# A mixing product in quarters of the array, with POOL making one of its later terms

## The reference

```
x, B, C = silu(conv(norm(u) @ W_in))           # x: 64 tokens x 512 channels
Y[l, h, p] = sum_s  (C[l] . B[s]) * L[h, l, s] * (x[s, h, p] * dt[s, h])      # L: decay, 0 for s > l
y = Y + x * D[h]
y = rmsnorm(y * silu(z)) * norm_w @ W_out
```

## Time and profile before

| | |
|---|---|
| median of 3 runs | 1300.21 us |
| the profiled execution | 1300.34 us, its span 1298.4 us |
| TensorE busy | 1229.9 us, 95% |
| VectorE busy | 1031.4 us, 79% |
| POOL busy | 796.1 us, 61% |
| ScalarE busy | 703.5 us, 54% |
| mean granted clock of TensorE | 0.978 |
| mixing product (L1278), 512 records | 35.9 us busy |
| mask product (L911, L914), 32 each | 21.5 and 22.1 us busy |
| first half of the gate (L928), 128 operations | 35.9 us busy |

### The profile page before, as it was taken

How to read it: one execution, slowest core, us unless ns; L and a number is a source line. 1 busy time by engine, 2 the same in 40 slices (tenths; PEclk the granted TensorE clock), 3 DMA queues, 4 the chain that set the end, 5 groups by cost and what they waited for, 6 DMA issues and landing times.

```text
span 1298.4 us, 32119 instructions
## 1 busy us (share of the span) xinstructions
PE 1229.9 (95%) x10803; PEld 1024.4 (79%) x10803; DVE 1031.4 (79%) x2572; ACT 703.5 (54%) x1588; POOL 796.1 (61%) x1435
## 2 busy tenths in 40 slices
PE   4789999999999999999999999999999999999865
PEld 3677888888888888888888888888888888888743
DVE  3675888888888888888888888888888888888555
ACT  3564566555555655555565555556555555665432
POOL 3465666667666666766666676666667666666541
PEclk8799999999999999999999999999999999999986
DMA  8300000000000000000000000000000000000000
GB/s 272 112 13 13 10 14 18 16 12 16 16 8 12 16 16 12 16 16 8 12 16 16 12 16 16 9 11 16 16 12 16 16 12 8 12 14 13 6 5 9
DMA packets 30645, 28.62 MB, mean 22 GB/s; under 512 B 7696, under 2 KB 28944, under 8 KB 30352
## 3 DMA queue, kind: packets, MB, share of 16 engines
q1 hardware_dynamic: 27680, 28.11, 6.8%
q10 hardware_dynamic: 2928, 0.03, 0.1%
HBM read 23.93 MB, written 4.19 MB: 22 GB/s over the span
## 4 chain that ended last, share of the span: by engine, by line
PE 87%; DVE 5%; POOL 3%; issue 2%; ACT 1%; DMA 1%; POOLq 0%; DVEq 0%; SPq 0%; ACTq 0%
PE bank L1405 17%; PE bank L1315 16%; PE bank L1397 5%; PE bank L1238 5%; PE bank L1375 4%; PE bank L1288 4%; PE bank L1247 4%; PE bank L1278 3%; PE bank L1425 3%; PE bank L1210 2%; PE bank L1430 2%; PE bank L1328 2%; PE bank L1227 2%; PE bank L1443 2%; PE bank L1385 2%
## 5 line engine op out<-in xcount | busy, mean ns | idle before, releaser
L1315 PE MATMUL bank<-xcT,wq 128*128 128x128 f32 x2048 | 236.2, 276 | 1.6 <-ACT xcT L648 1.6
L1315 PEld LDWEIGHTS bank<-xcT,wq 128*128 128x128 f32 x2048 | 231.1, 192 | 6.2 <-issue 2.0
L1405 PE MATMUL bank<-wo,oT 128*128 128x256 f32 x1024 | 232.1, 380 | 0.0
L1405 PEld LDWEIGHTS bank<-wo,oT 128*128 128x128 f32 x1024 | 190.6, 191 | 23.9 <-issue 0.3
L877 DVE SCALAR_TENSOR_TENSOR xc<-bank,cw,xc 128x124 f32<-128x124 f32 (+2 forms) x576 | 163.9, 341 | 15.2 <-ACT xc L618 8.4
L663 ACT ACTIVATE qT<-bank,bqT 128x128 f32<-128x128 f32 x384 | 109.7, 369 | 47.1 <-PE bank L1315 46.8
L354 POOL TENSOR_SCALAR m_mv<-m_mv 128x1 f32<-128x1 f32 x32 | 7.7, 241 | 158.1 <-DVE m_mv L845 158.1
L422 POOL TENSOR_TENSOR rq<-rq,minus_half 128x16 f32<-128x16 f32 x32 | 93.1, 2909 | 7.8 <-DVE rq L975 7.8
L1031 DVE SCALAR_TENSOR_TENSOR h<-h,bank 128x512 f32<-128x512 f32 x64 | 44.1, 688 | 64.9 <-ACT h L702 64.9
L434 POOL TENSOR_TENSOR pr<-pr,mask 128x512 f32<-128x512 f32 x64 | 82.9, 1315 | 14.0 <-DVE pr L982 14.0
L444 POOL TENSOR_TENSOR pr<-pr,mx 128x512 f32<-128x512 f32 x64 | 65.4, 1044 | 40.3 <-DVE mx L994 40.3
(11 more groups left out here) (225 smaller groups left out, 3053.7 us busy)
## 6 DMA issues: line engine op xcount, KB each, us to landing
x_in<-in_x SPq DMA_DIRECT2D x32, 128.0 KB, 2.1
c_in<-in_ctx SPq DMA_DIRECT2D x32, 128.0 KB, 2.0
x_m<-in_x SPq DMA_DIRECT2D x32, 128.0 KB, 2.0
out<-x SPq DMA_DIRECT2D x32, 128.0 KB, 1.7
wq<-in_L_xattn_Wq SPq DMA_DIRECT2D x1, 2048.0 KB, 14.3
wo<-in_L_xattn_Wo SPq DMA_DIRECT2D x1, 2048.0 KB, 12.7
w_in<-in_L_attn_W_in SPq DMA_DIRECT2D x1, 1024.0 KB, 6.0
qT<-in_L_ffn_w_gate SPq DMA_DIRECT2D x1, 1024.0 KB, 9.4
```

What stands on the lines that cost most here:

```text
L1315: last = mm(x_Qbank[g][:, (n % 4) * P:(n % 4 + 1) * P], wq[:, c, n * HD:(n + 1) * HD], xcT[:, c, :], start=(c == 0), stop=(c == DC - 1))
L1405: last = mm(X1[:, 0:D], oT[:, n, :, :], wo[:, n, :], start=(n == 0), stop=(n == NH - 1))
```

## The change

- `mbd` (128 x 8 x 128 with its zeros) becomes `mw` (128 x 8 x 64), the same weights without zeros; one multiplication of all 128 partitions writes it, and it now waits for the product of the tile before. The fill at the start goes.
- The product is made in 16 pieces. Each takes the 64 rows of one sequence, 64 columns of `xdt` and 64 of `mw`; the four pieces of a pair of heads lie on the four quarters of the array. The first sequence's results go to the first half of bank `M0`, the second's to the second half of bank `M2`. TensorE increments a semaphore that nobody waits for between the waits and the first piece.
- x * D becomes a product of POOL (`m_skip`, 128 x 512, into `xd`), after the attention's scaling and before `f_scales`; the gate adds it in two operations, one for each sequence. POOL's wait for D's load moves up with it, and VectorE's goes.
- As `M2` now holds results, `x_sums` waits for `m_y` (the gate's addition) instead of `m_Xdt`.

```diff
-            g.memset(mbd[:], 0.0).then_inc(s["c_memset"].sem, 1)
-            pool.wait_ge(s["c_memset"].sem, 5)
+            pool.wait_ge(s["c_memset"].sem, 4)
...
+        m_mixed = [M0[:, 0:2 * P], M2[:, 2 * P:4 * P]]
...
+            def m_skip(t):
+                after(pool, s["m_xs"], t + 1)
+                after(pool, s["m_y"], t)
+                g.tensor_tensor(xd[:], xc[:, 0:XCH, :], bcast(d_ch[:, :].unsqueeze(2), [P, XCH, P]),
+                                ALU.mult).then_inc(s["m_xd"].sem, 1)
...
+                if first == 0:
+                    pool.wait_ge(s["w_skip"].sem, 16 * W_SKIP)
+                if m is not None:
+                    m_skip(m)
                 if f is not None:
                     f_scales(f)
...
-                v.tensor_tensor(mbd[0:SEQ, :, 0:SEQ], decay[0:SEQ, :, :],
-                                bcast(gm[0:SEQ, :].unsqueeze(1), [SEQ, NHM, SEQ]), ALU.mult)
-
-                v.tensor_tensor(mbd[SEQ:P, :, SEQ:P], decay[SEQ:P, :, :],
-                                bcast(gm[SEQ:P, :].unsqueeze(1), [SEQ, NHM, SEQ]), ALU.mult).then_inc(s["m_Ma"].sem, 1)
+                after(dve, s["m_Y"], t)
+                v.tensor_tensor(mw[:], decay[:], bcast(gm[:, :].unsqueeze(1), [P, NHM, SEQ]), ALU.mult).then_inc(s["m_Ma"].sem, 1)
...
-                for j in range(XCH):
-                    last = v.scalar_tensor_tensor(out=yT[:, j, :], in0=xc[:, j, :], scalar=d_ch[:, j:j + 1],
-                                                  in1=M0[:, j * P:(j + 1) * P], op0=ALU.mult, op1=ALU.add)
+                after(dve, s["m_xd"], t + 1)
+                for a in range(2):
+                    tokens = slice(a * SEQ, (a + 1) * SEQ)
+                    last = v.tensor_tensor(yT[:, :, tokens], m_mixed[a].rearrange("p (j l) -> p j l", j=XCH), xd[:, :, tokens], ALU.add)
...
-                for n in range(NHM):
-                    last = mm(M0[(n % 2) * HP:(n % 2 + 1) * HP, (n // 2) * P:(n // 2 + 1) * P], xdt[:, n, :], mbd[:, n, :],
-                              start=True, stop=True)
+                pe.sem_inc(s["p_waited"].sem, 1)
+                for j in range(XCH):
+                    for a in range(2):
+                        rows = slice(a * SEQ, (a + 1) * SEQ)
+                        for u in range(2):
+                            last = mm(m_mixed[a][u * HP:(u + 1) * HP, j * SEQ:(j + 1) * SEQ], xdt[rows, 2 * j + u, :],
+                                      mw[rows, 2 * j + u, :], start=True, stop=True)
...
-                    after(pe, s["m_Xdt"], m + 1)
+                    after(pe, s["m_y"], m + 1)
```

More of the change, by code:

```diff
@@ L131, in decoder_layer @@
         gm = sb("gm", [P, SEQ])
-        mbd = sb("mbd", [P, NHM, P])
+        mw = sb("mw", [P, NHM, SEQ])
+        xd = sb("xd", [P, XCH, P])
         xdt = sb("xdt", [P, NHM, HP])
@@ L200, in decoder_layer @@
           m_raw+m_rl+m_nabs m_u m_up+m_rec+m_ratio m_log m_dt+m_dtA m_dAh+m_dAl m_Rh+m_Rl m_seg m_E m_tz m_zs
-          m_tap m_convb+m_conva m_tb+m_ta m_bc+m_xs m_G m_Gm+m_Ma m_Xtr m_Xdt
+          m_tap m_convb+m_conva m_tb+m_ta m_bc+m_xs m_G m_Gm+m_Ma m_Xtr m_Xdt m_xd
           m_Y m_y+m_yf m_sq m_ssy m_v4+m_ry m_out m_x1
@@ L504, in body @@
                     pool.wait_ge(s["w_out_l"].sem, 16)
-                    pool.wait_ge(s["w_skip"].sem, 16 * W_SKIP)
                     g.tensor_tensor(w_out[:], w_out[:], bcast(nw[:, :].unsqueeze(2), [P, XCH, D]),
@@ L1114, in body @@
                     m_spread(ms)
-                if first == 0:
-                    dve.wait_ge(s["w_skip"].sem, 16 * W_SKIP)
                 if m is not None:
```

## The result

| | before | changed |
|---|---|---|
| median of the runs, us | 1299.91 (1298.71 to 1300.24, 4) | 1284.15 (1283.53 to 1285.03, 4) |
| ratio, 95% interval | | 0.9881 [0.9864, 0.9898] |
| profiled execution, its span, us | 1300.34, 1298.4 | 1283.53, 1281.8 |
| a pass in the steady part, us | 37.80 | 37.41 |
| mixing product, start to next start, us | 1.02 | 0.63 |

The account below looks back on a forecast made before the run. TensorE's own time or its short idle gaps bound the kernel. Gains of 9.9 over 29 passes, 0.6 at the start and 1.1 in passes 0 to 2, 11.6 together, gave 1288.6 us, range 1284.5 to 1298.

Parts of the forecast that it names:

- The wait before the product, and the product: TensorE's mixing product: its wait for `mbd` goes, gain 0.26 a pass; the product takes 0.64 for 1.02, gain 0.38.
- The eight rounds: Mixing product with all four quarters at once: 8 rounds at 0.058 each beyond the first two, 0.64 in all.
- the other two orders: Mixing product with quarters two at a time, 16 rounds, 1.08; or one at a time, about 2.0.
- The ceiling of `f_qT`: Before L1425 (`f_up(0)`), which needs ScalarE's copy `f_qT`: a pass can gain at most 0.36 ahead of it.
- `xd` before `mw`: POOL's product starts at 663.0 or behind `f_norm`, ends before `mw`: cost 0, the other end 1.02.
- The sums' new wait for `m_y`: TensorE's `x_sums` (L1328): `m_y` comes 1.9 us before the sums start, so the wait costs nothing.
- The gate: VectorE's gate: two operations, 0.8 for 1.12, hidden behind L1031, cost and gain nothing.
- For passes 0 to 2 I take 0.38 each, 1.1.: First three passes: each gains 0.38, 1.1 in all.
- Start: I take 0.6.: Kernel start: POOL's 0.96 fill of `mbd` goes; between 0 and 0.96 is passed on, 0.6 taken.
- up to 0.5 late: Pass 0: POOL's product of `w_out` stands behind `xd` and may meet `mw`, up to 0.5 late.

Follow-up runs that it names:

- e2: The changed kernel with the sixteen quarter products reordered, all eight of the first sequence before all eight of the second: 1286.13 us.
- e6: The changed kernel with the 16 quarter products issued quarter by quarter, four in a row on each: 1304.16 us.
- e3: The changed kernel with ScalarE's square of the last query group moved behind the copy `f_qT`: 1275.48 us.
- e9: The kernel before with one edit, ScalarE's square of the fourth query head issued behind the copy `f_qT`: 1298.68 us.
- e10: The changed kernel with ScalarE's square behind the copy `f_qT` and the quarter products issued one sequence after the other: 1283.81 us.
- e8: The changed kernel with POOL's product `xd` issued behind `f_scales` instead of ahead of it: 1288.71 us.
- e1: The changed kernel with its mask product again made in two instructions of 64 partitions: 1289.75 us.
- e7: The changed kernel without POOL's product `xd`; VectorE's gate takes x times D itself in 8 instructions of 128x64: 1288.93 us.
- e5: The changed kernel with one more fill on POOL, of a spare tile, waited for at the start: 1285.33 us.
- e12: The changed kernel with ScalarE's square behind the copy `f_qT` and, in pass 0 alone, POOL's product of `w_out` ahead of `xd`: 1274.69 us.
- e11: The changed kernel with the mask in two instructions and the gate in 8 instructions without POOL's product: 1294.45 us.
- e4: The kernel before, unchanged, profiled once more: 1300.4 us.

## Why the prediction was right in the way and short in the size

- *The wait before the product, and the product.* Right: 0.26 and 0.39 for 0.26 and 0.38. The eight rounds follow each other by some 58 ns, the 0.058 of the forecast; they take 0.48 from the first start to the last, and the next stage comes 0.15 later. What was wrong is the count of rounds for the other two orders (e2, e6), and with it their sizes, 0.91 and 1.47 for 1.08 and about 2.0. By the Trainium skill, "TensorE: Matmul & The Clock Gate", section "Wait — 56ns, not 53.3ns?", starts would have stayed 25 ns apart; here 32 records began within 0.63 us, some 20 ns apart on average and 7 ns within a round, so the measurement decides against it for four quarters in turn.
- *The ceiling of `f_qT`.* Right, by e3, e9, e2 and e10. The forecast put L1425 0.10 behind `f_qT`; the 28 passes gave 0.38 each for 0.34 to 0.36.
- *`xd` before `mw`.* Right: L846 was first and `mw` 0.69; e8 shows the price of the other place.
- *The sums' new wait for `m_y`.* Right in the steady pass: the gate's first half ends at 658.57 and the sums start at 660.48, the 1.9 that the prediction left. In pass 2 of e1 and e7 TensorE does wait there, 0.9 and 1.0, but still waits another 0.3 for `m_sq` behind it.
- *The gate.* Failed. "It hides behind L1031, which waits for ScalarE anyway, and costs and gains nothing" is true in the steady pass (e7: 37.41). In passes 1 and 2 TensorE has idle time and the chain runs through VectorE's gate; there its 0.37 less were worth an estimated 0.4 each (e7).
- *"For passes 0 to 2 I take 0.38 each, 1.1."* This is the mis-sized term: it measured 5.06. I carried the steady pass's price into passes with another limit, without reading their waits. Pass 2 alone gave 2.96: about 1.55 from a stretch at half clock that is gone, the remaining 1.4 from mask and gate (1.0 by e1, an estimated 0.4 by e7). Pass 1 gave 0.76, half by the product and half by the gate, which waits for it there: from the product's start to the end of the gate's first half it took 2.25 before and 1.51 after, 0.37 of that the shorter gate and 0.37 the earlier end of the product. The other traces bear it out: e2's product, 0.28 longer, made pass 1 0.28 longer, and e7's gate, 0.87 longer, 0.89. Pass 0 gave 1.34. Of it 0.4 can be read at its end, where the next product comes 1.68 behind the start of `xdt` for 2.08, the mask being shorter; what the rest is made of stays open, for the stretches at half clock of the start lie differently in it from trace to trace.
- *"Start: I take 0.6."* Failed, -0.82 up to the first product. 0.45 is a later landing of the load, which e5 shows to be none of the fill's doing; the rest is `mw` behind `w_out`'s product, 1.76 where the two halves had taken 1.38, which the prediction named ("up to 0.5 late"); e12 takes it away. The first product comes 20.77 behind the landing for 20.40. Whether the shorter product makes that up in pass 0, as the prediction had it, is not shown.
- *The last stretch* had no term. From the last mixing product to the end it took 100.7 to 102.0 in the five traces with 26.3 to 27.4 us of half clock in it (changed, e3, e8, e10, e11), 103.2 to 103.7 in the five with 30.2 to 30.5 (before, e4, e2, e5, e7) and 104.4 to 105.4 in the four with 33.7 to 34.0 (e1, e6, e9, e12). So a half-clock stretch of 3.4 us costs 2.0 from the first group to the second and 1.3 from the second to the third, about 1.6, and the changed kernel's execution had one less than the kernel before. At equal clock the edits bring nothing there: e2, e5 and e7 took no less than the kernel before.

Forecast and result are 4.5 us apart in medians, 5.1 in the profiled spans. Of the latter an estimated 1.55 is the clock in pass 2 and 1.8 the end, 0.7 the steady passes; the remaining 1.0 is the chain of passes 0 to 2, through product, mask and gate, less the start. Open is how far the clock's part belongs to the change. In pass 2 the drop came in all five traces with a long gate (1.11 or 1.61: before, e4, e9, e7, e11) and in none of the nine with the short one (0.74), which speaks for it, though e5 and e6 had stretches of it in pass 1 instead. For the end nothing was found that decides which stretches fall.

## What to carry to other kernels

Price each stretch by its own last wait: what hides in the steady pass can be the chain in the first passes. When a term ends at a ceiling, name who sets the ceiling and move that in the same step: here one ScalarE instruction was worth 8.7 us after the change and nothing before it. And when a kernel has idle holes at its start or end, put one or two half-clock stretches into the range, on both sides; here one cost 0.6 to 2.0 us.

## What the runs showed of the hardware

- Quarters of 64x64: 16 f32 products (32 records of 64 columns) took 0.63 us issued round all four quarters, 0.91 over two at a time, 1.47 quarter by quarter. Only the order of issue differs between the three.
- A one-input VectorE operation (L1031, 256 columns in 0.34) stood still behind POOL's product for 0.8 us in e8, while a reduction of one input beside the same POOL product (L1020 in the changed kernel) kept its 0.42. The Trainium skill, "SBUF — State Buffer", section "Who interferes with whom", says that a tensor-scalar operation may take the shared ports in its fast mode and a reduction never does: the traces agree.
- In 21 runs the kernel before took 1295.6 to 1296.1 at a mean granted clock of 0.981 to 0.982, 1297.9 to 1301.0 at 0.977 to 0.979 and 1302.7 to 1304.7 at 0.973 to 0.975. The clock and the time go together over 9 us of a 1300 us kernel.
